# A four-layer conditioned transformer stack on one core: layer three's low parts by GpSimd, a ring of six PSUM banks, and another order for layer two

## The reference, cut to what matters

```python
# layer 1: x += attention(tc_rmsnorm(x)); x += swiglu(tc_rmsnorm(x)), hidden 1024
# layer 2: attention with biases, each head scaled by a sigmoid "coherence"
#          and mixed with a field; out @ Wout.T + bout
# layer 3:
scores = jnp.where(mask, -jnp.inf, (q @ k.T) * scale)   # per head
out = (softmax(scores) @ v) @ Wo.T
xn = out / rms(out) * rms_scale
x = x + xn * (1.0 + sc[:, None, :]) + shift[:, None, :]  # sc, shift from the conditioning
```

## Time and profile before

| | us |
|---|---|
| median of three runs (lowest, highest) | 1528.32 (1528.09, 1529.13) |
| the profiled execution | 1526.98 |
| its span, first to last instruction | 1525.2 |
| TensorE busy | 1445.9 (95%) |
| VectorE, ScalarE, GpSimd busy | 1094.8, 711.7, 264.5 |
| period of a batch in layer one, two, three | 41.24, 23.88, 22.74 |
| layer three's low part on VectorE (L523), each | 0.685 |
| the modulation row's copy on VectorE (L613), each | 0.686 |
| `norm` on VectorE (L573), each | 0.425 |

### The profile page before, as it was taken

How to read it: one execution, slowest core, us unless ns; L and a number is a source line. 1 busy time by engine, 2 the same in 40 slices (tenths; PEclk the granted TensorE clock), 3 DMA queues, 4 the chain that set the end, 5 groups by cost and what they waited for, 6 DMA issues and landing times.

```text
span 1525.2 us, 29475 instructions
## 1 busy us (share of the span) xinstructions
PE 1445.9 (95%) x10235; PEld 1199.9 (79%) x10283; DVE 1094.8 (72%) x3688; ACT 711.7 (47%) x1555; POOL 264.5 (17%) x322
## 2 busy tenths in 40 slices
PE   2669999999999999999999999999999999999997
PEld 1457888888888888888888787887877878887885
DVE  7747666666666666665666767777678888898886
ACT  1336333434444444333435555555555555555554
POOL 7401000000000000000112232322321111111112
PEclk9879999999999999999999999999999999999999
DMA  7056233332223232222224546354463454564450
GB/s 284 1 75 90 40 50 50 50 49 44 43 37 50 50 50 44 38 58 39 43 43 78 74 61 79 56 73 73 58 83 65 77 94 79 78 93 82 78 90 22
DMA packets 101132, 100.00 MB, mean 66 GB/s; under 512 B 11494, under 2 KB 97640, under 8 KB 100346
## 3 DMA queue, kind: packets, MB, share of 16 engines
q1 hardware_dynamic: 100986, 98.14, 38.8%
HBM read 16.83 MB, written 4.19 MB: 14 GB/s over the span
## 4 chain that ended last, share of the span: by engine, by line
PE 84%; DVE 6%; DMA 5%; issue 2%; ACT 2%; SPq 1%; POOL 0%; ACTq 0%; DVEq 0%; POOLq 0%
PE bank L1245 15%; PE bank L1104 13%; PE bank L1193 11%; PE bank L1183 10%; PE bank L1206 10%; PE bank L1253 7%; PE bank L1232 5%; PE bank L1112 5%; DMA ks<-qk_lo 4%; PE bank L1191 3%; PE bank L1120 2%; DVE ot_raw L428 1%; DVE work L427 1%; ACT work L997 1%; SPq L681 1%
## 5 line engine op out<-in xcount | busy, mean ns | idle before, releaser
L997 ACT ACTIVATE work<-bank 128x512 f32<-128x512 f32 x768 | 450.2, 598 | 298.5 <-PE bank L1193 238.4
L541 DVE TENSOR_REDUCE rowmax<-bank 128x2 f32<-128x512 f32 x512 | 339.2, 679 | 121.4 <-PE bank L1183 121.2
L1193 PE MATMUL bank<-qs,ks 98*128 98x256 f32 x1536 | 411.8, 351 | 5.0 <-DVE rowmax L541 4.4
L1183 PE MATMUL bank<-ks,qs 96*128 96x256 f32 x1536 | 321.1, 291 | 10.7 <-DMA ks<-qk_lo 10.5
L1193 PEld LDWEIGHTS bank<-qs,ks 98*128 98x128 f32 x1536 | 274.0, 191 | 54.5 <-issue 11.5
L1183 PEld LDWEIGHTS bank<-ks,qs 96*128 96x128 f32 x1536 | 241.1, 190 | 24.6 <-DMA ks<-qk_lo 14.3
L538 DVE CUSTOM_DVE_ANT_0 c1t<-bank,big_q 128x256 bf16<-128x256 f32 x512 | 192.8, 421 | 0.7
L1206 PE MATMUL bank<-work,vp 128*32 128x256 f32 x3072 | 185.7, 382 | 0.0
L1023 ACT ACTIVATE work<-bank 128x256 f32<-128x256 f32 x128 | 49.1, 383 | 236.2 <-PE bank L1245 236.2
L1206 PEld LDWEIGHTS bank<-work,vp 128*32 128x32 f32 x3072 | 90.0, 109 | 65.4 <-issue 5.0
L1245 PE MATMUL bank<-yt,w_gate 128*128 128x256 f32 x512 | 131.8, 379 | 0.4 <-ACT yt L1017 0.3
(11 more groups left out here) (220 smaller groups left out, 1751.2 us busy)
## 6 DMA issues: line engine op xcount, KB each, us to landing
qs<-qk_hi SPq DMA_DIRECT2D x192, 128.0 KB, 4.0
ks<-qk_hi SPq DMA_DIRECT2D x192, 128.0 KB, 3.7
qs<-qk_lo SPq DMA_DIRECT2D x96, 128.0 KB, 4.5
ks<-qk_lo SPq DMA_DIRECT2D x96, 128.0 KB, 4.3
xres<-in_x_t SPq DMA_DIRECT2D x4, 1024.0 KB, 9.0
x_in<-in_x SPq DMA_DIRECT2D x16, 256.0 KB, 2.8
out<-xres SPq DMA_DIRECT2D x15, 256.0 KB, 2.9
qs<-nm SPq DMA_DIRECT2D x96, 16.0 KB
```

The costliest lines, as they stand in the source:

```text
L541: a = dve.tensor_reduce(rowmax[:, :, k:k + 1], bank[:, :].rearrange("p (t s) -> p t s", t=TC), AX, ALU.max)
L997: act.activation(probs[:, place[n, b, k], :, :], bank[:, :].rearrange("p (c s) -> p c s", c=TC), ACT.Exp, scale=HD ** -0.5)\
L1183: m = pe.matmul(bank[:, t * S:(t + 1) * S], qs[par][0:SCORE_ROWS, k, t * P:(t + 1) * P], ks[par][0:SCORE_ROWS, k, :], start=True, stop=True)
L1193: m = pe.matmul(bank[:, c * S:(c + 1) * S], ks[par][0:SHIFTED_ROWS, k, c * P:(c + 1) * P], qs[par][0:SHIFTED_ROWS, k, :], start=(n != 3), ...
```

## The change

- Layer three's `q` and `k`: ScalarE makes a second, unrounded copy of the bank (`qk_full`, in the unused half of layer one's `w_down`), and GpSimd instead of VectorE subtracts `qk_hi` from it. The bank is free after ScalarE's copy.
- The modulation row is copied out of `acc_bank` by ScalarE instead of VectorE, and `mod` moves from slot 14.36 to 16.57.
- The ring has six banks; `pv` has the seventh for itself, and its first matmul waits for the last turning out of it.
- Layer three has two more buffers for exponentials (14 in all), in the other half of `w_down`.
- `SLOT` and `LATER` change in all layers. In layer two `k` comes 1.36 slots later, `neg` 0 a slot earlier, the stack of k 0.83 earlier and pv 2 and 3 a slot later; in layer one `yn` comes 1.72 slots earlier and ffn 0.83; in layer three `q` comes 1.49 and `k` 3.32 slots later.
- Steps `cap` and `expo` are written for heads in `BESIDE`, which is empty, so none is issued.

```diff
-        "smax": -13.9, "pv": (8.3, 16.3), ..., "neg": (-6.41, 1.59),
-        "max": (-6.11, 4.35), "xT": -26.32, ..., "yn": 23.31,
-        "yT": 24.38, "ffn": (26.56, 1.11), "down": (28.62, 1.18)},
+        "smax": -13.9, "pv": (8.3, 16.3), ..., "neg": (-6.41, 2.26),
+        "max": (-6.29, 4.51), "xT": -26.99, ..., "yn": 21.59,
+        "yT": 24.38, "ffn": (25.73, 1.11), "down": (27.4, 1.24)},
     2: {
-        "smax": -14.72, "pv": (9.43, 16.22), ..., "neg": (-6.46, 1.15),
-        "max": (-6.72, 2.71), ..., "stack": (-23.72, -21.22, -15.9, -15.63), "k": -24.09,
+        "smax": -14.72, "pv": (9.43, 17.26), ..., "neg": (-7.45, 1.15),
+        "max": (-6.52, 2.71), ..., "stack": (-23.72, -22.05, -15.9, -15.63), "k": -22.73,
     3: {
-        ... "q": -24.57, "stack": (-24.46, -20.12, -14.49, -15.03), "k": -23.17, "v": -13.11,
-        "mod": 14.36, "oT": 17.22, "wo": 20.21, "squares": 23.07, "resid": 24.6},
+        ... "q": -23.08, "stack": (-24.04, -19.29, -15.9, -15.03), "k": -19.85, "v": -12.83,
+        "mod": 16.57, "oT": 16.94, "wo": 20.71, "squares": 22.54, "resid": 24.6},
...
-        head = middle = back = Ring(sem("banks_full"), banks[0:7])
+        head = middle = back = Ring(sem("banks_full"), banks[0:6])
...
-                    return [(head, what, self.qk_lo, "qk".index(what) + 1)]
+                    return [(head, what, full_ok if self.n == 3 else self.qk_lo, "qk".index(what) + 1)]
...
+                    if what in ("q", "k") and n == 3:
+                        side = "qk".index(what)
+                        part = slice(DC * side, DC * (side + 1))
+                        pool.wait_ge(full_ok.sem, full_ok.at(b, side + 1))
+                        pool.wait_ge(L.stacked[DC - 1].sem, L.stacked[DC - 1].at(b, 0))
+                        pool.tensor_tensor(qk_lo[:, part, :], qk_full[:, part, :], qk_hi[:, part, :], ALU.subtract).then_inc(L.qk_lo.sem, 1)
...
+                        if n == 3:
+                            act.wait_ge(L.qk_lo.sem, L.qk_lo.at(b - 1, side + 1))
+                            act.copy(qk_full[:, DC * side:DC * (side + 1), :], bank[:, :].rearrange("p (c s) -> p c s", c=DC)).then_inc(full_ok.sem, 1)
...
+                        act.wait_ge(mod_full.sem, mod_full.at(b, 1))
+                        act.copy(x_in[:], acc_bank[:, :].rearrange("p (a d) -> p a d", a=2)).then_inc(mod_ok.sem, 1)
...
-                        bank = head.bank(n, b, f"pv{k // 2}")
-                        if k % 2 == 0:
-                            head.wait_free(pe, n, b, f"pv{k // 2}")
+                        if k % 2 == 0 and not (n == 1 and b == 0 and k == 0):
+                            pe.wait_ge(L.o_raw.sem, L.o_raw.at(b, k // 2))
```

More of the change, by code:

```diff
@@ L30 @@
 MORE = 4
+MOST = 2
+BESIDE = ()
 HALF = H // 2
@@ new lines @@
+        "max": (-6.29, 4.51), "xT": -26.99, "q": -24.35, "stack": (-25.3, -22.08, -15.97, -16.88), "k": -22.83, "v": -12.2,
+        "load": -46, "rank": -32.95, "cond": -30.74, "squares": -28.63, "xn": -28.27, "oT": 18.5, "wo": 21.54, "yn": 21.59,
+        "yT": 24.38, "ffn": (25.73, 1.11), "down": (27.4, 1.24)},
+    2: {
+        "smax": -14.72, "pv": (9.43, 17.26), "rz": (9.93, 17.56), "norm": (14.07, 17.86), "neg": (-7.45, 1.15),
+        "max": (-6.52, 2.71), "xT": -26.47, "q": -24.49, "stack": (-23.72, -22.05, -15.9, -15.63), "k": -22.73, "v": -11.32,
+        "load": -30, "coh1": -13.18, "coh2": -10.81, "coh3": -10.48, "vsum": 1.0, "sumv": 4.81, "field": 5.63, "oT": 19.5,
@@ L50 @@
         "wo": 22.05},
     3: {
-        "smax": -13.86, "pv": (9.2, 15.39), "rz": (9.7, 15.69), "norm": (11.29, 15.39), "neg": (-6.26, 3.29),
-        "max": (-6.13, 2.38), "xT": -26.55, "q": -24.57, "stack": (-24.46, -20.12, -14.49, -15.03), "k": -23.17, "v": -13.11,
-        "mod": 14.36, "oT": 17.22, "wo": 20.21, "squares": 23.07, "resid": 24.6},
+        "smax": -13.86, "pv": (9.2, 15.39), "rz": (9.7, 15.69), "norm": (12.06, 15.36), "neg": (-5.51, 3.12),
+        "max": (-6.13, 2.38), "xT": -26.55, "q": -23.08, "stack": (-24.04, -19.29, -15.9, -15.03), "k": -19.85, "v": -12.83,
@@ L122, in plan @@
             out += [(at + h, what, h) for h in range(H)]
+        elif what in ("cap", "expo"):
+            out += [(at + h, what, h) for h in range(H) if h % HALF in BESIDE]
         elif what in ("ffn", "down"):
@@ L131, in plan, with beside @@
     return out
+def beside(b, k):
+    return (b * DC + k // HALF) * len(BESIDE) + sum(h < k % HALF for h in BESIDE)
 def schedule(engine):
@@ L155, in probs_buffers @@
                 ring = list(range(PBUF, PBUF + MORE)) + ring
+            if (n, b) == (3, 0):
+                ring = list(range(PBUF + MORE, PBUF + MORE + MOST)) + ring
             for h in range(H):
@@ L382, in run_layers, with probs_tile @@
                 steps[n](what, k, b, b % 2)
+        def probs_tile(n, b, h):
+            i = place[n, b, h]
+            return probs[:, i, :, :] if i < PBUF + MORE else w_down[:, TC * (i - PBUF - MORE):TC * (i - PBUF - MORE + 1), :]
         def rows(name, n):
@@ L511, in step @@
                             dve.tensor_scalar(xn[:, t, :], xres[:, b, t, :], stat[:, 2, t:t + 1], None, ALU.mult).then_inc(xn_ok.sem, 1)
-                    if what in ("q", "k"):
+                    if what in ("q", "k") and n < 3:
                         side = "qk".index(what)
@@ L994, in step @@
                             act.wait_ge(lay[n_was].pv.sem, lay[n_was].pv.at(b_was, k_was // HG + 1))
-                        elif n == 2:
+                        elif n > 1:
                             act.wait_ge(down_part.sem, down_part.at(NBATCH, 0))
-                        act.activation(probs[:, place[n, b, k], :, :], bank[:, :].rearrange("p (c s) -> p c s", c=TC), ACT.Exp, scale=HD ** -0.5)\
-                            .then_inc(L.probs.sem, 1)
+                        tile, scores = probs_tile(n, b, k), bank[:, :].rearrange("p (c s) -> p c s", c=TC)
+                        if n == 3 and k % HALF in BESIDE:
+                            act.copy(tile, scores).then_inc(L.probs.sem, 1)
+                        else:
+                            act.activation(tile, scores, ACT.Exp, scale=HD ** -0.5).then_inc(L.probs.sem, 1)
                     if what == "wo" and n == 2:
@@ L1205, in step @@
                                 j = HG * k + i
[L1206 to L1209, removed]
+                                m = pe.matmul(pv_bank[HW * i:HW * (i + 1), (k % 2) * S:(k % 2 + 1) * S], vp[par][:, c, DC * (j % HALF) + j // HALF, :],
+                                              probs_tile(n, b, j)[:, c, :], start=(c == 0), stop=(c == TC - 1))
                         m.then_inc(L.pv.sem, 1)
```

45 lines of the change are left out of this document (25 added, 20 removed).

## The result

The changed kernel takes **1539.61 us** (median of 4 runs, 1539.35 to 1541.87) where the kernel before takes 1528.20 on the same chip: a ratio of 1.0078 [1.0066, 1.0090], slower by 11 us. Forecast were 1525.1 and a range up to 1537.5, so the time lies outside it, on the slow side. The profiled execution took 1539.54, its span 1537.8, 12.6 more than before, at the same mean granted clock of 0.989.

A forecast was written before the change was run, and what follows sets the result against it. TensorE was taken to bound layers one and three, with waits on VectorE and k's low part in layer two. Terms -11.6, +4.2, +4.5 and at most -0.3 for the tail took 1528.3 to 1525.1 us; eight in ten: 1514 to 1537.5.

The forecast's parts named there:

- Layer two's other order: Layer two: the new order shortens VectorE's queue and lands k's low part earlier; 0.9 us gained per batch, -11.6 us.
- The rival that the shorter ring takes back what the order frees: Layer two: heads 14 and 15 wait for heads 11 and 12, so no gain; 1537.0 us, chance 0.1.
- Layer one: Layer one: `yn` ahead of heads 4, 5 and q's low part delays k's matmuls; 0.32 us per batch, +4.2 us.
- Layer three's low parts: Layer three: k's low part lands 8.1 us after k's start, with 7.9 available; 0.3 us per batch, +4.5 us.
- My upper bound of 4.25 a landing: Layer three: with layer two's landing time, k's low part arrives at 8.65 us; 0.85 per batch, +12.8 us.
- The third rival: Layer three, head 0 of every batch: k's low part lands later, as in layer two; 1533.7 us, chance 0.2.
- The fourth rival: Layer three: GpSimd's subtraction of k waits for VectorE's `norm`, 425 ns by 15 batches, 6.4 us; 1531.5 us, chance 0.1.
- 9 points: Layer three, a sign: VectorE's busy share falls by some 9 points at no gain.

## Why the prediction was wrong, step by step

**Layer two's other order: right.** 0.73 a batch in place of 0.9. The total, -10.4 against -11.6, is nearer than that by luck: 12 batches at 0.73 are 8.8, and 1.6 are two long batches of the kernel before, which the prediction did not look at. The rival that the shorter ring takes back what the order frees has a part in it: the two kernels before with the new order show 0.96 with seven banks and 0.73 with six. It was given a chance, but only as the whole of the gain.

**Layer one: right, in place, size and cause.** +4.7 against +4.2, and `yn` at its old slot removes it; 3.9 of it are eleven batches of 0.35 each, the rest is in the first two. The rows that answer to the earlier trace rows: `yn` runs while GpSimd adds, low q comes behind two maxima, and k's matmuls behind low q:

```profile
396.40 1.62 DVE L608 TENSOR_SCALAR yn<-y,statb 128x256 f32<-128x256 f32 x2 [2.02 <-POOL statb L854]
397.94 1.28 DVE L558 TENSOR_REDUCE rowmax<-bank 128x2 f32<-128x512 f32 x2
...
399.14 0.68 DVE L540 TENSOR_TENSOR qk_lo<-bank,qk_hi 128x512 fp32r<-128x512 f32 x1
...
399.96 1.97 PE L1141 MATMUL bank<-xt,wqkvo 128*128 128x256 f32 x8
```

Low q ends at 399.82, 3.42 after the start of `yn` where the prediction had 3.44, and k's matmuls start 0.15 behind it in each batch from 180 to 590 us, for 0.95 before. TensorE's waits by name list none of this there: they leave it at an idle time of 0.26 before the first weight load, put down to no one.

VectorE stood idle for 2.02 us with the maxima of heads 4 and 5 behind `yn` in its queue: the price is of the queue's order, not of work.

**The overlap of layers one and two: not in the prediction.** I read three steady stretches and priced nothing between them; it cost 5.0, of it 1.7 by the clock. With layer two's order alone it is 3.4, 1.7 of it by the clock again (half speed from 773.0, a microsecond after a wait of 2.3 for `yn`), and TensorE waits at the transposes of `yn` and once for q's low part (before, for `yn` once, 0.6). Both rows are from 590 to 840 of that kernel:

```profile
PE bank L1120 <- DVE yn L591: 2.7, 2, 2.3
PE bank L1193 <- DVE qk_lo L519: 0.9, 1, 0.9
```

These waits lie in it; which slot of layer two causes them was not tested. The start's -1.6 and the end's -1.1 stay open too.

**Layer three's low parts: this step failed.** Everything up to the issue was right: the matmuls, both copies on ScalarE, 1.28 for GpSimd's subtraction, 4.38 us for 4.4. In a clean batch the landing was 3.7 and the loss 0.3, as worked out. The mis-sized term is the landing: "here it follows by 1.8. So it lands at 8.1". One row of 3.7 us stood for all batches. The mean of the 13 was 4.4, and the loss 1.18 a batch, 1.05 without the clock's 1.7. My upper bound of 4.25 a landing came from one row of layer two, and gave +12.8, so even the bound lay below the 15.4, and below the 13.7 without the clock. The clock's share, 1.7 here and 1.7 in the overlap, is a term that the prediction did not have at all; the landing's 9.5 us are the larger miss. The third rival named the place, the wait and the point from which it decides; its reason (a low part close behind its high ones) is what the kernel with VectorE's low parts does show, at 4.2 to 4.3, but it isn't what happened here. The question that I did not ask: how does the landing of this copy spread over all batches. The row of 3.7 was of another copy, `qs<-qk_lo`; k's own for heads 0 to 7 stood in the trace before with 4.2 to 4.3 in 11 batches and 5.0 in two, both beside a packet of 16 KB. A path moved to where it has 7.9 us for 8.1 must be priced with the spread, for there late copies cost in full (the table above).

**GpSimd and VectorE: right direction, wrong way round.** The fourth rival had GpSimd's subtraction wait for `norm`. The subtraction kept to 1.27 to 1.29, and `norm` grew instead. Before and after, 1180 to 1500 (times ns, min, median, max):

```profile
L573 DVE TENSOR_TENSOR on<-ot_raw,rz x29: 417/424/426, 1180.4 to 1496.8; 128x256 f32<-128x256 f32 x29
```

```profile
L590 DVE TENSOR_TENSOR on<-ot_raw,rz x27: 831/1442/1472, 1182.0 to 1493.1; 128x256 f32<-128x256 f32 x27
```

So VectorE's share of layer three fell only from 85.43 to 84.66 where I expected 9 points: about a microsecond, twice a batch, went into standing still. No wait for `norm` shows on TensorE. The rule quoted in the prediction (the Trainium skill, SBUF — State Buffer, SBUF: two separate sides: whichever starts first keeps the shared ports for its whole instruction) holds: GpSimd's subtraction began at 1200.34, `norm` at 1200.71, and ended 0.27 after it.

## What to carry to other kernels

- Before a step is moved towards its deadline, ask for the spread of its transfer over all batches; with no slack left, the time is the mean of what lies beyond the deadline, not the median landing. One slot of slack (a pair of score steps, 0.7 us) was worth 10 us here, of the whole time.
- A change of many edits is best priced and tried apart: the order of layer two alone gives -0.6%, and the edits that came with it took that and 0.8% more.
- Read the overlaps between the stages as well as the steady stretches; 5 us came from there.
- When a ledger leaves something over, look at the granted clock of that very stretch: a mean of 0.989 in both kernels hid 3.4 us.

## What the runs showed of the hardware that was not expected

- TensorE's code arrives in packets of 16 KB that occupy one of the 16 DMA engines for about 1.5 us, and other code in packets of 8 KB for about 0.8 us. A 128 KB copy between buffers on the chip that otherwise took 3.7 us took 5.0 to 5.3 where one of the first kind came within 1.3 us of its issue, 4.6 where it came 2.7 after (with one of 8 KB before it), and 4.1 to 4.5 with one of the second kind. With k one slot earlier, packets of 16 KB that came 1.7 and 2.0 us after the issue left it at 3.7.
- Of three such copies issued one behind the other the last landed about 5.5 us after the first was issued, whether it was issued 1.2 or 1.8 us behind it.
- A VectorE product of two tiles in SBUF of 0.42 us took up to 1.47 beside a GpSimd instruction of 1.28, which itself was not slowed.
- Between 110 and 1500 us TensorE's granted clock fell to half for 3.4 us at a time (twice 6.8) in nine of the twelve kernels, each time during a wait of 0.9 to 2.3 us or within 3 us behind it. Most waits as long left it full, and what decides was not tested.
